# Target loop in laps of six gathers, one-hots loaded in two parts, and VectorE subtracting the middle part for two of three

## The reference

```
def _gnn_layer(nf, traj, src, dst, We, be, Wn, bn):
    ef = jnp.concatenate([nf[src], nf[dst], traj[:, None]], axis=-1)
    msg = jax.nn.leaky_relu(ef @ We.T + be, negative_slope=0.01)
    red = jax.ops.segment_sum(msg, dst, num_segments=nf.shape[0])
    h = jnp.concatenate([nf, red], axis=-1)
    return jax.nn.leaky_relu(h @ Wn.T + bn, negative_slope=0.01)
x = _layernorm(x + L0(x, ..., src, dst))
h = x
for We, be, Wn, bn in params:      # three layers
    h = _gnn_layer(h, edge_weight, src, dst, We, be, Wn, bn)
x = _layernorm(x + h)
```

## Time and profile before

| | us |
|---|---|
| runs, median (lowest, highest) | 11125.28 (11124.88, 11136.86) |
| the profiled execution, its own time | 11117.06 |
| its span | 11115.9 |
| target loop of layers 1, 2, 3, from first add to last | 1485.85, 1465.17, 1418.67 |
| PE, DVE, ACT, POOL busy | 9122.6, 8733.7, 7420.3, 4178.1 |

### The profile page before, as it was taken

How to read it: one execution, slowest core, us unless ns; L and a number is a source line. 1 busy time by engine, 2 the same in 40 slices (tenths; PEclk the granted TensorE clock), 3 DMA queues, 4 the chain that set the end, 5 groups by cost and what they waited for, 6 DMA issues and landing times. The chain is left out here.

```text
span 11115.9 us, 545161 instructions
## 1 busy us (share of the span) xinstructions
PE 9122.6 (82%) x201170; PEld 7772.2 (70%) x201170; DVE 8733.7 (79%) x16671; ACT 7420.3 (67%) x19555; POOL 4178.1 (38%) x4286
## 2 busy tenths in 40 slices
PE   7999997549976666599878778998888899888887
PEld 6999997326765555588666666886666678766665
DVE  6999998458989999788666667886666678767667
ACT  7888884016669999676666666766666667666665
POOL 0000001570008887344444443444444434444442
PEclk9999998559999999799999999999999999999998
DMA  1000000125658888499766665987676759877774
GB/s 43 8 8 9 8 8 8 36 46 189 209 192 255 254 256 247 125 293 293 214 205 209 205 201 162 294 279 213 208 212 209 210 181 294 266 218 221 216 215 142
DMA packets 1299036, 1961.63 MB, mean 176 GB/s; under 512 B 192608, under 2 KB 831082, under 8 KB 1297258
## 3 DMA queue, kind: packets, MB, share of 16 engines
q1 hardware_dynamic: 1052054, 1285.20, 35.2%
q0 software_dynamic: 245248, 650.66, 21.8%
q10 hardware_dynamic: 304, 4.93, 0.1%
HBM read 1225.54 MB, written 719.25 MB: 175 GB/s over the span
## 5 line engine op out<-in xcount | busy, mean ns | idle before, releaser
L1827 POOL DMA_INDIRECT work<-rows,oct_at x1752 | 1963.8, 1121 | 2447.4 <-DVE work L1952 2357.0
L1661 PE MATMUL bank<-work 128*128 128x64 bf16 x56064 | 2141.4, 195 | 234.7 <-issue 211.5
L1952 DVE TENSOR_TENSOR work<-bank,work 128x512 f32<-128x512 f32 x1752 | 1210.0, 691 | 1411.5 <-PE bank L1903 1376.9
L1903 PEld LDWEIGHTS bank<-work 128*128 128x128 fp8e4 x42048 | 1509.6, 100 | 1019.3 <-issue 679.5
L1661 PEld LDWEIGHTS bank<-work 128*128 128x128 fp8e4 (+1 forms) x56064 | 1905.9, 99 | 303.9 <-issue 282.5
L1903 PE MATMUL bank<-work 128*128 128x64 bf16 x42048 | 1615.4, 196 | 533.4 <-issue 348.7
L1605 PE MATMUL bank<-work 128*128 128x64 bf16 x34560 | 1565.1, 193 | 6.2 <-issue 6.2
L1605 PEld LDWEIGHTS bank<-work 128*128 128x128 fp8e4 x34560 | 1409.8, 98 | 173.0 <-issue 6.3
L1859 ACT CAST work<-bank 128x512 bf16<-128x512 f32 x1752 | 1038.2, 593 | 471.3 <-issue 456.5
L1853 ACT CAST work<-bank 128x512 bf16<-128x512 f32 x1752 | 1038.3, 593 | 351.3 <-issue 252.4
L1624 DVE TENSOR_SCALAR work<-bank,part 128x512 fp8e4<-128x512 f32 x1440 | 1026.7, 750 | 283.5 <-PE bank L1585 283.0
(11 more groups left out here) (363 smaller groups left out, 20045.2 us busy)
## 6 DMA issues: line engine op xcount, KB each, us to landing
work<-hits_g SPq DMA_DIRECT2D x1752, 256.0 KB
rows<-work SPq DMA_DIRECT2D x1440, 256.0 KB, 3.2
hits_g<-work SPq DMA_DIRECT2D x584, 256.0 KB
rows<-work SPq DMA_DIRECT2D x480, 260.0 KB
work<-hits_s SPq DMA_DIRECT2D x720, 128.0 KB, 3.1
work<-rows,oct_at POOLq DMA_INDIRECT x2336
hits_s<-work SPq DMA_DIRECT2D x240, 128.0 KB
side<-meta POOLq DMA_DIRECT2D x720, 20.0 KB, 3.1
```

The costliest lines, as they stand in the source:

```text
L1661: last = ten.matmul(to[:, 0:D], hits_of(j), piece_of(j), start=j == 0 and k == 0, stop=j == OCT - 1 and k == 2, skip_group_check=True)
L1827: pool.indirect_dma_start(octs[g % ROWS], None, table_octs, bass.IndirectOffsetOnAxis(ap=oct_at[:, g:g + 1], axis=0)).then_inc(s_octs[g % ...
L1903: last = ten.matmul(to[:, j * D:(j + 1) * D], hits_t[:, j * P:(j + 1) * P], window[q % WINDOWS][:, k * D:(k + 1) * D], start=j == 0 and k ...
L1952: vec.tensor_tensor(total[g % 2], z[g % BANKS][:, :], octs[g % ROWS], ALU.add).then_inc(s_added, 1)
```

## The change

Laps of the target loop shrink from 24 to 6 gathers, with 12 gathers alone ahead of the loop (`alone` = 2), 94 laps in it and 8 gathers alone behind it. The one-hots of a gather come as two transfers of 128 KB, each into six buffers of its own: the turned half waits for `before_message` of g - 6, the upright half for the scatter of g - 6. Rows, windows and low parts have six buffers instead of four. For gathers with g % 3 > 0, VectorE makes the low part as bank minus middle part in one subtraction, which waits for the middle part; for these gathers the matmul `less_mid` is not issued. For g % 3 == 0 `less_mid` and a cast by ScalarE stay. The window registers are loaded six at a time instead of four. The semaphores of the row stores are shared by the first source loop and the later ones, so their counts start elsewhere.

```diff
-    def laps(engine, count, step, size=LAP):
-        for q in range(size):
-            step(q, q, 0)
-        with engine.Fori(1, count // size - 1) as i:
+    def laps(engine, count, step, size=LAP, alone=1):
+        for g in range(alone * size):
+            step(g, g % size, g // size)
+        with engine.Fori(alone, count // size - 1) as i:
...
-        s_out = [sem_of(f"rows_out{n}", False) for n in range(MADE)]
+        s_out = [sem_of(f"rows_out{n}", True) for n in range(MADE)]
...
-        AROUND, HITS, ROWS, WINDOWS, BANKS, MIDS, LOWS = 24, 8, 4, 4, 6, 6, 4
+        TURNED, UPRIGHT, ROWS, WINDOWS, BANKS, MIDS, LOWS = 6, 6, 6, 6, 6, 6, 6
...
-        pairs_done = lambda lap, q: past * NG // 2 + lap * (AROUND // 2) + q // 2 + 1
+        by_vector = lambda g: g % 3 > 0
+        like = lambda g, count: sum(by_vector(n) == by_vector(g) for n in range(count))
+        lows_made = lambda lap, q: past * like(q, NG) + (lap + q // AROUND) * like(q, AROUND) + like(q, q % AROUND + 1)
...
-                at_least(syn, s_sum, g - HITS + 1, since)
-                syn.dma_start(hits_home[q % HITS], hits_g[bass.ds(g, 1), :, :]...)
+                at_least(syn, s_before, g - TURNED + 1, since)
+                syn.dma_start(hits_turned[q % TURNED]..., hits_turned_at[bass.ds(g, 1), :, :]...)
+            def load(g, q):
+                at_least(syn, s_sum, g - UPRIGHT + 1, since)
+                syn.dma_start(hits_home[q % UPRIGHT]..., hits_at[bass.ds(g, 1), :, :]...)
             def step(g, q, lap):
-                load(g + HITS - 1, q + HITS - 1)
+                load_turned(g + TURNED - 1, q + TURNED - 1)
+                load(g, q)
...
-                if q % 4 == 0:
-                    next_windows[:] = registers(sca, win_g[0:1, bass.ds(g, 4)], NW - 1)
+                if q == 0:
+                    next_windows[:] = registers(sca, win_g[0:1, bass.ds(g, ... AROUND)], NW - 1)
                 window_of(g, q)
-                if begun(g, LESSER + 3) and (q - LESSER - 3) % 2 == 0:
+                if begun(g, LESSER + 3) and not by_vector(q - LESSER - 3):
                     low_of(...)
...
-            def scatter(g, q, low_made):
-                ten.wait_ge(s_low[q % 2], low_made)
+            def scatter(g, q, lap, low_made):
+                ten.wait_ge(s_in[q], since_in[q] + 16 * (lap + 1))
+                ten.wait_ge(s_low[by_vector(q)], low_made)
...
-                if begun(g, LESSER):
+                if begun(g, LESSER) and not by_vector(q - LESSER):
                     less_mid(g - LESSER, (q - LESSER) % AROUND)
-            laps(ten, NG, step, AROUND)
+            laps(ten, NG, step, AROUND, 2)
...
             def low_of(g):                                    # VectorE
                 at_least(vec, s_sum, g - LOWS + 1, since)
-                vec.wait_ge(s_lesser, since + g + 1)
-                vec.tensor_copy(low[g % LOWS], z[g % BANKS][:, :]).then_inc(s_low[1], 1)
+                vec.wait_ge(s_mid, since + g + 1)
+                vec.tensor_tensor(low[g % LOWS], z[g % BANKS][:, :], mid[g % MIDS], ALU.subtract).then_inc(s_low[True], 1)
...
-                if g % 2 and LOW <= g < NG + LOW:
+                if LOW <= g < NG + LOW and by_vector(g - LOW):
                     low_of(g - LOW)
```

More of the change, by code:

```diff
@@ L1578, in side_here @@
                 n = q // GROUP_LOT % SIDES
-                ten.wait_ge(s_side[n], since_out + (lap + 1) * 16)
+                ten.wait_ge(s_side[n], since_side + (lap + 1) * 16)
                 return sides[n][:, q % GROUP_LOT, :]
@@ L1791, in target_phase @@
         s_octs = [sem_of(f"sums_octs{n}", True) for n in range(GATHERED)]
-        AROUND, HITS, ROWS, WINDOWS, BANKS, MIDS, LOWS = 24, 8, 4, 4, 6, 6, 4
-        s_in = [sem_of(f"sums_in{n}", True) for n in range(HITS)]
+        TURNED, UPRIGHT, ROWS, WINDOWS, BANKS, MIDS, LOWS = 6, 6, 6, 6, 6, 6, 6
+        s_in = [sem_of(f"sums_in{n}", True) for n in range(UPRIGHT)]
+        s_in_turned = [sem_of(f"sums_in_turned{n}", True) for n in range(TURNED)]
         s_window, s_before, s_added, s_leaky, s_high, s_less, s_mid, s_lesser, s_sum, s_kept = (
@@ L1799, in target_phase @@
         past = number - 1
-        since, since_octs, since_in = past * NG, number * (NG // GATHERED) * 16, past * (NG // HITS) * 16
+        since, since_octs = past * NG, number * (NG // GATHERED) * 16
+        since_in = [past * 16 * len(range(n, NG, AROUND)) for n in range(AROUND)]
         room = Room(work, WORK)
         octs = [room.cut(OCT * D) for _ in range(ROWS)]
-        hits_home = [room.cut(OCT * P // 2, BF16) for _ in range(HITS)]
+        hits_turned = [room.cut(OCT * P // 4, FP8) for _ in range(TURNED)]
+        hits_home = [room.cut(OCT * P // 4, FP8) for _ in range(UPRIGHT)]
         window = [room.cut(3 * D // 2, BF16) for _ in range(WINDOWS)]
@@ L1868, in window_of @@
                 at_least(sca, s_before, g - WINDOWS + 1, since)
[L1869 removed]
+                sca.copy(window[q % WINDOWS].unsqueeze(1), tabs[:, 1, bass.ds(next_windows[q], 1), :]).then_inc(s_window, 1)
             def step(g, q, lap):
[L1872 to L1873 removed]
+                if q == 0:
+                    next_windows[:] = registers(sca, win_g[0:1, bass.ds(g, min(AROUND, NG - g) if isinstance(g, int) else AROUND)], NW - 1)
                 window_of(g, q)
[L1875 to L1876 removed]
+                if begun(g, LESSER + 3) and not by_vector(q - LESSER - 3):
+                    low_of(g - LESSER - 3, (q - LESSER - 3) % AROUND, lows_made(lap, q - LESSER - 3))
                 if begun(g, LESS + 3):
@@ L1880, in step @@
                     high_of(g - 3, (q - 3) % AROUND)
-            laps(sca, NG, step, AROUND)
+            laps(sca, NG, step, AROUND, 2)
             for g in range(NG, NG + LESSER + 3):
-                if (g - LESSER - 3) % 2 == 0:
-                    low_of(g - LESSER - 3, (g - LESSER - 3) % AROUND)
+                if not by_vector(g - LESSER - 3):
+                    low_of(g - LESSER - 3, (g - LESSER - 3) % AROUND, lows_made(0, g - LESSER - 3))
                 if g - LESS - 3 < NG:
@@ L1931, in step @@
                 if begun(g, SCATTER):
-                    scatter(g - SCATTER, (q - SCATTER) % AROUND, pairs_done(lap, q - SCATTER))
+                    scatter(g - SCATTER, (q - SCATTER) % AROUND, lap - (q < SCATTER), lows_made(lap, q - SCATTER))
                 if begun(g, LESS):
                     less_high(g - LESS, (q - LESS) % AROUND)
-                if begun(g, LESSER):
+                if begun(g, LESSER) and not by_vector(q - LESSER):
                     less_mid(g - LESSER, (q - LESSER) % AROUND)
-            laps(ten, NG, step, AROUND)
+            laps(ten, NG, step, AROUND, 2)
             for g in range(NG, NG + SCATTER):
-                scatter(g - SCATTER, (g - SCATTER) % AROUND, pairs_done(0, g - SCATTER))
+                scatter(g - SCATTER, (g - SCATTER) % AROUND, (g - SCATTER) // AROUND, lows_made(0, g - SCATTER))
                 if g - LESS < NG:
                     less_high(g - LESS, (g - LESS) % AROUND)
-                if g - LESSER < NG:
+                if g - LESSER < NG and not by_vector(g - LESSER):
                     less_mid(g - LESSER, (g - LESSER) % AROUND)
```

28 lines of the change are left out of this document (17 added, 11 removed).

## The result

The changed kernel takes 10633.05 us (median of 4 runs, 10619.77 to 10634.37), the kernel before 11126.2 us beside it: ratio 0.9552, 95% interval 0.9536 to 0.9569. It is faster by 493 us. The forecast was 10330, so the change gave 62% of the 796 us forecast. The execution profiled after took 10633.43 us.

The account below looks back on a forecast made before the run. Target loops were held by TensorE's instruction refetch at lap ends and a chain between engines. Saving 570 us of lap ends and 219 of pace: 11117 - 4370 + 3581 = 10328, said 10330; forecast 10,230 to 10,450, 8-in-10 range 10,050 to 10,680.

Parts of the forecast that it names:

- the second rival: Target loops: pace stays at 2.16 or rises, from transfers or successive lows delaying each other; 10,550 to 10,800 us; chance 0.22.
- no refetch: Target-loop lap ends: laps of 6 end TensorE's instruction refetch; branch 0.2 us median, packets from 265 to under 60.
- the 570 us of the lap ends: Target loops: gain from removing the cost of 66 lap ends, 8.6 us each.
- undisturbed pace: Target loops: steady pace without lap ends, two gathers in 4.31 us, 2.155 each.
- cross-check: Target loop outside laps: 2.1 us a gather over 56 gathers, so straight code streams at the steady pace.
- the 219 us of the pace: Target loops: gain from a faster gather after VectorE's subtraction, 1752 x 0.125 us, at a forecast 2.03 us a gather.
- the chain, 1.66 + 1.94 + 1.52 + 0.915 = 6.04: Target loops: message, two adds with lows, scatter, next message; longest cycle of three gathers, 2.01 us each.
- The wait on which it turns: Before the target loops' scatter: TensorE waits for VectorE's low part and addition into `hr` in two of three steps.
- TensorE's cycle (5.06 for three): Target loops: TensorE's own work for three gathers, 1.83 + 2 x 1.615 = 5.06 us.
- VectorE's (5.22): Target loops: VectorE's own work for three gathers, 1.94 + 1.94 + 1.34 = 5.22 us, 1.74 a gather.
- expected cover for its new wait: VectorE's subtraction: the middle part it waits for is ready over a microsecond ahead, so the wait costs nothing.
- two pauses of 6.1: Each target lap end before: TensorE stands still 4.26 us before the first matmul, 1.84 us again after 15.

Follow-up runs that it names:

- e5: Changed kernel with both one-hot transfers bringing only 16 of 128 partitions, an eighth of the bytes (wrong sums): ratio 0.9567 to the kernel before.
- e3: Changed kernel with VectorE's low part of an earlier gather placed ahead of the add instead of behind it: 10573.22 us, ratio 0.9534 to the kernel before.
- e2: Changed kernel with target laps of 24 gathers again, everything else of the change kept: 10995.52 us, ratio 0.991 to the kernel before.
- e1: Changed kernel without VectorE's subtraction: low parts cast by turns on VectorE and ScalarE, second TensorE subtraction for every gather: 10696.42 us, ratio 0.9645 to the kernel before.
- e10: Changed kernel with VectorE subtracting for every gather and its low part ahead of the add: 10282.23 us, ratio 0.924 to the kernel before.
- e11: Changed kernel with VectorE subtracting for every gather, VectorE's order as in the change: 9980.68 us on a quicker chip, ratio 0.9232 to the kernel before.
- e12: Changed kernel with one gather of six by TensorE and ScalarE, low part ahead of the add: 9870.12 us on a quicker chip, ratio 0.913 to the kernel before.
- e4: Changed kernel with the scatter's one-hot weights read from consecutive bytes instead of every second element (wrong sums): ratio 0.9572 to the kernel before.
- e6: Changed kernel with ScalarE loading window registers for three gathers at a time instead of six: ratio 0.9586 to the kernel before.
- e9: Changed kernel with VectorE's and ScalarE's operations on the messages cut to 64 of 512 columns, all waits kept: 10305.0 us, ratio 0.9259 to the kernel before.
- e7: Changed kernel with the scatter leaving out the low part, 16 matmuls instead of 24: 10439.95 us, ratio 0.9416 to the kernel before.
- e8: Changed kernel with VectorE only counting the semaphore instead of making low parts; the scatter reads the middle part twice: 10507.47 us, ratio 0.9481 to the kernel before.

## Why the prediction was right or wrong

**Right: faster, and in the range.** 10633 lies in 10,050 to 10,680, near its upper end, and outside the forecast's own 10,230 to 10,450. The number is that of the second rival (a pace that stays at 2.16 or rises, 0.22), at 2.22; its price at that pace is 1752 x 2.22 + 24 = 3913 us for the loops, against 3894 measured. Neither of its two causes was borne out: an eighth of the bytes of the hits changes nothing (e5), and low parts ahead of the add change the pace by 0.03 (e3). So it was the width of the range that held the result, not the working: the lap ends were priced at 1.4 times what they gave and the pace at twice, and the range was wide enough for both misses. That is luck.

**Right: no refetch.** The branch takes 215 ns, with 7 packets. The Trainium skill ("Runtime: NRT & Kernel Launch", "Instruction fetch mechanics") gives TensorE room for 2048 instructions; the trace agrees, as a lap of some 630 jumps in 0.2 us and one of over 2400 in 4.3. Its other statement, that only two blocks are held, is not borne out for TensorE by this lap, which would be longer than two blocks of 256.

**Too large: the 570 us of the lap ends.** e2 against the change measures 398. The term was everything above an undisturbed pace, and that pace was taken from one quiet pair of gathers, 2.155. It is not the mean of laps without a refetch: that is 2.264 (e1). The prediction's own cross-check, 2.1 us a gather outside the laps, rested on 56 gathers near the loop's ends. Of 313 us missed in the loops (3894 - 3581), 1752 x 2.264 - 3800 = 166 are this step, "straight code streams at the undisturbed pace".

**Too large: the 219 us of the pace.** The subtraction gave 0.93% by the ratios (103 us), and 70 us by the loops (1752 x 0.04, on two chips), so that this step missed by about 148 us in the loops. What failed is the chain, 1.66 + 1.94 + 1.52 + 0.915 = 6.04, as the thing that sets the pace: the loops take 6.67 for three. The wait on which it turns holds up 7% of the scatters and not two of three, and with 0.6 us of it taken away (e3) the pace moved by 0.03. TensorE's cycle (5.06 for three) and VectorE's (5.22) were worked out well: VectorE is busy for 1053.43/584 = 1.80 us a gather, forecast 1.81. Its 81% in place of 89% is the pace, not the work. So 1.4 of the 6.67 us lie in no engine's work, and 0.6 beyond the longest chain that the prediction had drawn.

**What took its place.** Shown: the loss comes with the gathers whose middle part TensorE subtracts and whose low part ScalarE casts, when there are two in a lap of six (e10, e11 and e12 against the change and e3). It is not the bytes of the hits (e5), the weights' layout (e4), the register loads (e6) or VectorE's order (e3, e11). It shrinks when VectorE and ScalarE have little to do (e9), and only by a part when TensorE (e7) or VectorE (e8) alone has less. Where TensorE loses the time can be counted from the starts of its matmuls in the second loop (gathers 30 to 560): each start that comes over 0.15 us later than in a dense stream (0.029 us after a matmul of 64 columns, 0.213 after one of 512), inside a block of 24 or between blocks. In us a gather:

| | pace | inside blocks | between blocks |
|---|---|---|---|
| change | 2.23 | 0.32 | 0.16 |
| e3, low part first | 2.20 | 0.33 | 0.15 |
| e1, no subtraction on VectorE | 2.27 | 0.08 | 0.32 |
| e9, narrow VectorE and ScalarE | 2.02 | 0.16 | 0.29 |
| e10, none of six by ScalarE | 2.01 | 0.11 | 0.37 |
| e11, the same (quicker chip) | 1.95 | 0.00 | 0.33 |
| e12, one of six (quicker chip) | 1.88 | 0.00 | 0.20 |

From e3 to e12 the pauses inside blocks go, 0.33 us, and the pace falls by about as much, 0.32 (some 0.05 of it is the chip). In the change they are two thirds of the late starts. But e1 has few of them and is the slowest of these: there TensorE is late between blocks, most of it (0.22) before the scatter. So these stops are not the loss in every form of the kernel. Not settled: what stops TensorE inside a block, and why two gathers per lap cost so much more than one. No event of another engine was found that ends the stops. The transfers of the gathered rows, and the place of the stops in the lap's code, were not varied by themselves.

**Right, and costing nothing:** two transfers of 1 KB lines need (0.404 + 0.395) x 1280/575 = 1.78 us of the queues a gather (forecast 1.74), 236 GB/s pass and 278 in e12, and within the loops TensorE waits for a transfer of hits twice, 0.2 us each, both in its weight loads (in the first loop before, its matmuls L1903 waited 36 times, for 24.8 us). The subtraction from PSUM costs 681 ns, as the cast did:

```profile
L1984 DVE TENSOR_TENSOR work<-bank,work 128x512 bf16<-128x512 f32 x1167 | 794.6, 681 | 4.0 <-ACT work L1874 4.0
```

The expected cover for its new wait held too: 4.0 us in three loops for ScalarE's middle part.

## What to carry to other kernels

Where a loop has a dear event at each turn, take the pace between the events from all laps (a row of the stretch from one end to the next, less the event's own pauses), and not from a quiet pair in the timeline: a quiet pair is the best case, and it makes the event look dearer and the rest cheaper than they are. Here the lap of 62.2 us less its two pauses of 6.1 gives 2.34 a gather, and the pair 2.155; 2.264 was measured without a refetch (e1), between the two. When no engine is full and every chain that you draw leaves time over, look for the step that differs from its neighbours and take it out, even at the price of more work for the busiest engine: here VectorE got 7% more to do and the kernel 3.3% faster. Sweep the split: of the three tried, none, one and two in six, the best was one.

## What the runs showed of the hardware

- A block of 24 dense matmuls can stop for 0.4 to 0.5 us after the modelled end of the one before, in most cases with no wait in the trace, at full clock (granted 0.99 to 1.00 in these loops). Stops of 0.5 to 0.8 us from start to start come 210 times in the second loop of the change, 282 times in e3's and 52 in e1's, 13 in e10's, 2 in e12's and none in e11's: one step of the program more or less makes them come and go.
- The semaphore of a block of matmuls can come late: 0.21 us after the start of its last matmul in one case above, 1.99 us in the next block, behind which the scatter stopped.
- The time of one load of window registers doesn't follow their number: 4 took 0.309 us in the median (the kernel before), 6 took 0.772 (the change) and 3 took 0.702 (e6). The last two (min/median/max ns):

```profile
L1270 ACTq TENSOR_LOAD <-win_g x294: 497/772/1367, 5264.3 to 10513.2; - x147
```
```profile
L1270 ACTq TENSOR_LOAD <-win_g x585: 488/702/731, 5260.2 to 10507.8; - x195
```

- The same program, the kernel before, took 10,806 us on one chip and 11,083 to 11,126 us on the others, 2.6 to 3.0% more; one of these gave 11,083 at one time and 11,125 at another. That is more than several of the steps that were to be told apart: only ratios to a kernel run beside it compare.
